# Loading and splitting the expert weights during the image attention instead of the linear attention

## The reference

```python
h = image_attention(x)                                  # 4 x 256 x 192
h = concatenate([h, txt], axis=1)                       # 4 x 384 x 192
h = h + linear_attention(layernorm(h))                  # q, k = elu(..)+1, gate, running sum of k (x) v, head norm
f = layernorm(h)
probs = softmax(f @ router_w.T); topk_probs, topk_idx = top_k(probs, 2)
outs  = einsum('tei,ehi->teh', silu(einsum('th,eih->tei', f, w1)), w2)
h = h + sum over the two chosen experts of balanced[k] * outs[topk_idx[k]]
```

## Time and profile before

| what | value |
|---|---|
| time, median of 3 runs | 404.68 us (402.76 to 408.04) |
| span of the profiled execution, first to last instruction | 391.4 us |
| median less span: what lies around it | 13.3 us |
| busy in the span: PE, DVE, ACT, POOL | 65%, 67%, 47%, 33% |
| mean granted TensorE clock | 0.711 |

### The profile page before, as it was taken

The page is one execution under the profiler, slowest core; times in us unless marked ns, Lnnn a source line. Parts: engine busy times, 40 slices in busy tenths (PEclk is TensorE's granted clock), DMA queues, the critical chain, the costliest instruction groups (busy, mean ns, idle before and its releaser), DMA issues.

```text
span 391.4 us, 7182 instructions
## 1 busy us (share of the span) xinstructions
PE 254.3 (65%) x2269; PEld 182.2 (47%) x2270; DVE 261.5 (67%) x763; ACT 184.2 (47%) x396; POOL 128.6 (33%) x133
## 2 busy tenths in 40 slices
PE   5986658776443334546656579512899999999800
PEld 3444434444343333435555457501376667667600
DVE  2115568997388898899949976597355555655566
ACT  1131325898798587657526321400255456445401
POOL 3000232554025423303300000012667876866321
PEclk9998556999555565555555555555699999999975
DMA  6000032000004512220100000000211211110046
GB/s 182 6 0 0 1 124 93 3 0 2 2 2 107 121 68 83 80 82 2 32 1 3 7 23 3 30 30 10 62 51 51 69 45 57 53 43 27 26 146 216
DMA packets 12973, 18.98 MB, mean 48 GB/s; under 512 B 3259, under 2 KB 10850, under 8 KB 12434
## 3 DMA queue, kind: packets, MB, share of 16 engines
q1 hardware_dynamic: 9922, 13.90, 11.8%
q0 software_dynamic: 3024, 4.73, 4.1%
HBM read 14.68 MB, written 5.41 MB: 51 GB/s over the span
## 4 chain that ended last, share of the span: by engine, by line
PE 43%; DVE 39%; issue 7%; ACT 6%; DMA 3%; SPq 1%; POOL 0%; DVEq 0%; POOLq 0%; ACTq 0%
DVE at_half L1434 6%; DVE atm L1397 5%; PE bank L891 4%; PE bank L880 3%; PE bank L904 2%; PE bank L906 2%; PE bank L905 2%; PE bank L741 2%; PE bank L876 2%; PE bank L578 2%; PE bank L879 2%; PE bank L878 2%; PE bank L877 2%; DVE v L1320 2%; PE bank L546 2%
## 5 line engine op out<-in xcount | busy, mean ns | idle before, releaser
L480 POOL TENSOR_TENSOR wx<-early,wx 128x1536 f16<-128x1536 f32 (+2 forms) x8 | 28.7, 3584 | 62.6 <-ACT wx L1075 62.6
L1116 ACT ACTIVATE qk<-bank 128x512 f32<-128x512 f32 x31 | 18.5, 597 | 65.1 <-PE bank L880 65.1
L487 POOL DMA_INDIRECT qk<-x_rows,tok_row x32 | 38.6, 1206 | 24.1 <-DVE tok_row L1550 12.8
L741 PE MATMUL bank<-vg,at_half 128*128 128x17 f16 x432 | 13.5, 176 | 40.8 <-DVE at_half L1434 40.8
L492 POOL DMA_INDIRECT y_rows<-qk,dst_row x31 | 31.4, 1013 | 21.7 <-DVE qk L1589 14.9
L1583 DVE COPY qk<-bank 128x512 f16<-128x512 f16 x31 | 13.2, 425 | 33.2 <-PE bank L891 33.2
L741 PEld LDWEIGHTS bank<-vg,at_half 128*128 128x128 f16 x432 | 12.5, 104 | 42.4 <-DVE at_half L1434 27.7
L904 PE MATMUL bank<-wx,qk 128*128 x124 | 30.5, 246 | 0.7 <-DVE qk L1583 0.5
L906 PE MATMUL bank<-wx,qk 128*128 x124 | 30.5, 246 | 0.0
L905 PE MATMUL bank<-wx,qk 128*128 x124 | 30.5, 246 | 0.0
L1056 ACT ACTIVATE at_half<-atm 128x384 f16<-128x384 f32 x48 | 22.5, 518 | 12.9 <-DVE atm L1397 12.9
(11 more groups left out here) (297 smaller groups left out, 737.0 us busy)
## 6 DMA issues: line engine op xcount, KB each, us to landing
early<-in_w SPq DMA_DIRECT2D x4, 768.0 KB, 4.2
early<-in_w1a SPq DMA_DIRECT2D x2, 1024.0 KB, 6.0
early<-in_w1b SPq DMA_DIRECT2D x4, 512.0 KB, 6.3
x_rows<-xr SPq DMA_DIRECT2D x12, 96.0 KB, 1.7
v<-y_rows SPq DMA_DIRECT2D x4, 288.0 KB, 5.0
qk<-y_rows SPq DMA_DIRECT2D x4, 288.0 KB, 5.3
out<-h SPq DMA_DIRECT2D x4, 288.0 KB, 2.9
at_half<-in_wq SPq DMA_DIRECT2D x1, 704.0 KB
```

Of the source, the lines that this page charges most:

```text
L480: pool.tensor_tensor(low, w, high, ALU.subtract).then_inc(s_w_low, 1)
L487: pool.indirect_dma_start(xg[:, i % 4, :], None, x2_dram, bass.IndirectOffsetOnAxis(ap=tok_row[:, i:i + 1], axis=0), bounds_check=NTOK - 1 ...
L741: mm = pe.matmul(bank[6][:, hh * VE:(hh + 1) * VE], at_half[:, a_, i, g, :], vg[:, t * H + hh, v, :], start=(c == 0 and hh == 0 and a_ == ...
```

## The change

Four stages take the place of two, and none of them lies in `early`: they are the places of `v32` (the values), `vg` (their halves), and the last two pieces of 2048 words of `qk` (queries and keys). All of these are written only in the projections. So the loads need to wait for nothing: SP issues the first four jobs directly behind the setup loads, the others when the job of four before is subtracted, and only then places the bias rows. ACT rounds each job in the image attention in one pass (scale and cast together). POOL now scales in place and then subtracts, for the jobs 0 to 3 ahead of the qkv low halves, for 4 to 6 ahead of `x_low(0)`, and for 7 between `x_low(1)` and `x_low(2)`. The subtraction of the jobs 2 and 3 covers 128 partitions as the others do. New waits: ACT waits for six subtractions before the projections, and for eight before tile 6 of them; DVE for six before it sets the ones and zeros of `vg`, which move from the start to tile 2; ACT for all key halves before the linear attention.

```diff
+NB = 4
+FREE_V = 6
+FREE_QK = 8
...
+        stage = (v32[:].rearrange("p t e -> p (t e)"), vg_words[:],
+                 late[:, T * H * SLOT - 2 * STG:T * H * SLOT - STG], late[:, T * H * SLOT - STG:T * H * SLOT])
...
-            sp.wait_ge(s_himg_mm, B)
             for n, (kind, e0) in enumerate(jobs):
-                if n >= 2:
-                    sp.wait_ge(s_w_low, n - 1)
+                if n >= NB:
+                    sp.wait_ge(s_w_low, n - NB + 1)
...
+            def expert_weights(n):
+
+                w, high, low = staged(n)
+                pool.wait_ge(s_w_high, n + 1)
+                link(pool.tensor_scalar(w, w, WS, None, ALU.mult))
+                pool.tensor_tensor(low, w, high, ALU.subtract).then_inc(s_w_low, 1)
+
+            for n in range(4):
+                expert_weights(n)
             pool.wait_ge(s_wqhigh_ready, 2)
...
+            for n in range(4, 7):
+                expert_weights(n)
...
             x_low(0)
             x_low(1)
+            expert_weights(7)
...
-            for n in range(len(jobs)):
-                w, high, low = staged(n, parts[jobs[n][0]][1])
-                pool.wait_ge(s_w_high, n + 1)
-                pool.tensor_tensor(low, w, high, ALU.subtract).then_inc(s_w_low, 1)
...
+            def expert_weights(n):
+
+                w, high, _low = staged(n)
+                act.wait_ge(s_w_loaded[n % NB], 16 * loads[n])
+                act.activation(high, w, ACT.Copy, scale=WS).then_inc(s_w_high, 1)
+
             softmax(0)
             softmax(1)
+            expert_weights(0)
+            expert_weights(1)
             for b in range(B):
                 himg(b)
                 if b + 2 < B:
                     softmax(b + 2)
+                if b == 0:
+                    expert_weights(2)
...
+                expert_weights(b + 3)
...
+            expert_weights(7)
+            act.wait_ge(s_w_low, FREE_V)
             for t in range(T + 2):
                 if t < T:
+                    if t == (T * H * SLOT - 2 * STG) // (H * SLOT):
+                        act.wait_ge(s_w_low, FREE_QK)
...
-                    act.activation(w, w, ACT.Copy, scale=WS).then_inc(s_w_scaled, 1)
...
-                    act.wait_ge(s_w_scaled, t + 1)
-                    act.activation(high, w, ACT.Copy).then_inc(s_w_high, 1)
...
+                if t == 2:
+                    dve.wait_ge(s_w_low, FREE_V)
+                    link(dve.memset(vg[:, :, 0, DH:VE], 1.0))
+                    link(dve.memset(vg[:, :, 1, DH:VE], 0.0))
```

More of the change, by code:

```diff
@@ L119, in build @@
         xp1 = qkT[:].rearrange("p a n -> p (a n)")[0:NP1, 0:B * NI]
-        early = sb("early", [P, 2 * STG])
-        stage = early[:].rearrange("p (b n) -> p b n", b=2)
+        early = sb("early", [P, 4 * IT * NI + B * IT * D])
         atm = sb("atm", [P, HG, G, P])
@@ L163, in build @@
         v32 = sb("v32", [P, T * H, DH])
-        vg = sb("vg", [P, T * H, 2, VE], F16)
+        vg_words = sb("vg", [P, T * H * VE])
+        vg = vg_words[:].bitcast(F16).rearrange("p (t v e) -> p t v e", v=2, e=VE)
         state = sb("state", [P, G * HG * VE])
@@ L304, in build @@
         s_x2_stored = [sem(f"x2_stored{i}") for i in range(2)]
-        s_w_loaded = [sem(f"w_loaded{i}") for i in range(2)]
-        s_w_scaled = sem("w_scaled")
+        s_w_loaded = [sem(f"w_loaded{i}") for i in range(NB)]
         s_w_high = sem("w_high")
@@ L353, in build @@
         jobs = [(k, e0) for k in parts for e0 in range(0, E, STG // parts[k][0])]
-        loads = [sum(2 if k == "w1b" else 1 for k, _ in jobs[n % 2:n + 1:2]) for n in range(len(jobs))]
+        loads = [sum(2 if k == "w1b" else 1 for k, _ in jobs[n % NB:n + 1:NB]) for n in range(len(jobs))]
+        assert len(jobs) == FREE_QK and all(n % NB > 1 for n in range(FREE_V, FREE_QK))
         def staged(n, rows=P):
@@ L360, in staged @@
             ne = STG // width
-            return (stage[0:rows, n % 2, 0:ne * width].rearrange("p (e c) -> p e c", c=width),
+            return (stage[n % NB][0:rows, 0:ne * width].rearrange("p (e c) -> p e c", c=width),
                     by_expert[0:rows, e0:e0 + ne, high:high + width], by_expert[0:rows, e0:e0 + ne, low:low + width])
@@ L404, in _ @@
                     for r in range(2):
-                        sp.dma_start(stage[r * 64:(r + 1) * 64, n % 2, 0:cols], w).then_inc(s_w_loaded[n % 2], 16)
+                        sp.dma_start(stage[n % NB][r * 64:(r + 1) * 64, 0:cols], w).then_inc(s_w_loaded[n % NB], 16)
                 else:
-                    sp.dma_start(stage[:, n % 2, 0:cols], w).then_inc(s_w_loaded[n % 2], 16)
+                    sp.dma_start(stage[n % NB][:, 0:cols], w).then_inc(s_w_loaded[n % NB], 16)
+            sp.wait_ge(s_wqhigh_ready, 2)
+            sp.wait_ge(s_biaslow_ready, 1)
+            for v in range(2):
+                sp.dma_start(w_half[D - P + v:D - P + v + 1, 1, 1, 0:3 * D], bias_half[:, v, :]).then_inc(s_bias_placed, 16)
             for t in range(T):
@@ L1048, in _ @@
             heads_t(1)
+            act.wait_ge(s_klow_ready, T)
             for t in range(T + 1):
@@ L1062, in _ @@
                     heads_t(t + 1)
-                if t < len(jobs):
-                    w, high, _low = staged(t)
-                    act.wait_ge(s_w_loaded[t % 2], 16 * loads[t])
-                    act.activation(w, w, ACT.Copy, scale=WS).then_inc(s_w_scaled, 1)
                 if 0 <= t - 4 < PT:
@@ L1181, in _ @@
             dve.memset(oT[DC:DC + 1, :, :, :], 1.0).then_inc(s_ones_ready, 1)
-            link(dve.memset(vg[:, :, 0, DH:VE], 1.0))
-            link(dve.memset(vg[:, :, 1, DH:VE], 0.0))
             dve.wait_ge(s_axt_mm, 1)
```

1 line of the change is left out of this document (removed).

## The result

| | before | after |
|---|---|---|
| time, median of 4 runs each, taken together | 404.66 us (402.76 to 408.04) | 435.79 us (435.22 to 437.54) |
| ratio, 95% interval | | 1.0758 (1.0687 to 1.0828) |
| span of the profiled execution | 391.4 us | 434.0 us |

The change makes the kernel 31.1 us slower. The forecast, 419 (404 to 431), has the sign and not the size.

What follows compares the result with a forecast made beforehand. VectorE (DVE) was taken to bound the linear attention, a chain of turns the image attention. Queue 14.2 + waits 13 + memsets 0.4 - linear attention 12.9 = +14.7 us, giving 419 us; 8 of 10 within 404 to 431.

Steps and rivals of the forecast that it cites:

- Part 1: Linear attention: eight subtractions leave GpSimd and VectorE's waits on them go, a gain of 12.9 us.
- Part 2: GpSimd's queue before the projections: scales of 2.0 and 1.55 us plus subtractions start `x_low(0)` at 70.7, 14.2 us later.
- Part 3: Image attention and norm chains: VectorE and GpSimd hold each other up in four places, 13 us together (0 to 17).
- job 7: Beside the second norm chain: its scale and subtraction stop the chain for most of 1.55 + 3.10, 2.5 us.
- The 3.5 us of the norm chain: First norm chain: its 17 instructions move one per GpSimd instruction; some fourteen left when GpSimd ends, some 3.5 us.
- The rest: Loads, ScalarE's first passes and its new waits cost nothing; VectorE's two memsets moved into the projections cost 0.4 us.
- The place of `x_low(0)` before: End of the image attention: GpSimd's first `x_low` read at 56.55 us, the start the delay was counted from.
- The 13.3 us between median and span: Whole kernel: time taken to lie around the 391.4 us span, added to the predicted span of 406.1 to give 419.4.
- Rival B: GpSimd's queue: the scale is as slow as the subtraction, 12.9 us more, 432 us; chance 0.13.
- A: Image attention: VectorE's waits cost nothing extra, GpSimd's queue alone decides, 406.4 us, no change; chance 0.22.
- C: Linear attention: a faster TensorE there; chance 0.10, a third of it together with A.
- D: Start of kernel: early loads come late, sharing rings with the setup; 4 us late gives 423 us; chance 0.05.

Runs made afterwards that it cites:

- e12: Kernel after, with GpSimd's scale replaced by a copy of the weights onto themselves: 406.52 us, ratio 1.0291 to the kernel before.
- e3: Kernel after without GpSimd's scale and subtractions, low halves set to zero in the setup: 392.25 us, ratio 0.9643 to the kernel before.
- e4: Kernel before without its eight subtractions, low halves set to zero in the setup: 393.26 us, ratio 0.967.
- e5: Kernel before, with each GpSimd subtraction cut in four instructions: 404.33 us, ratio 0.9943.
- e6: Also called the probe: kernel before plus seven GpSimd instructions on scratch, from 4.6 to 33.8 us; one run, 406.32 us, span 404.3.
- e10: Kernel before plus five unused subtractions on GpSimd from 27 us on; one run, 404.44 us against 396.42.
- e11: Kernel before plus four unused scales on GpSimd from 27 us on; one run, 407.79 us against 396.42.
- e13: Kernel after with the scale on GpSimd left out, so GpSimd only subtracts: 395.96 us, ratio 1.0015 to the kernel before.
- e9: Kernel before, with jobs 0 to 5 loaded early, cast by ScalarE in one pass, low halves made by VectorE while waiting for TensorE: 385.82 us, ratio 0.9738.
- e8: Kernel after, with GpSimd's scales and subtractions replaced by zero fills of about the same length: 422.51 us, ratio 1.0673 to the kernel before.
- e7: Kernel after, with each GpSimd scale and subtraction cut in four: 438.31 us, ratio 1.0861 to the kernel before.

## Why the prediction was wrong in size

By its own steps, each against the stages above:

- **Part 1, what goes from the linear attention: right.** Predicted -12.9, measured -13.0. L1320, L1325, L1361 and L1358 of the earlier trace rows are at 0.75 and 0.17 us. All of it was on the chain.
- **Part 2, GpSimd's queue in front of `x_low(0)`: the step that failed.** Its words: "From above, it should not be longer than the subtraction with two inputs, 4.07. I take 2.0 and 1.55". The scale took 5.37 and 4.08. That is 4 x 3.37 + 3 x 2.53 = 21.1 us more, and with 0.08 between each scale and its subtraction, seven times, 21.6: the queue's work ends at 92.4 without its pauses, not at 70.7. The bound was argued from the number of inputs. The only rows of GpSimd with one stream were fills, and the copy is indeed near them. An arithmetic operation with one input was not in the rows, and "from above" should have stayed open. The prediction had named this as a sign of being wrong: "if the scale takes under 1.5 or over 3 us".
- **Part 3, the waits in the image attention: right for the kernel that it thought of, hidden in the one that came.** It had 4 + 3 + 3.5 = 10.5 us of pauses in GpSimd's queue, and 2.5 for job 7. e12, where the second operation costs what was assumed, has 2.94 + 2.96 + 2.85 = 8.8, and 2.9 in the second norm chain, so each of the four was near by itself and not only their sum. The kernel after has 3.7, since the longer queue covers them. Job 7 beside the second norm chain was given 2.5 us and took 5.5: a scale and a subtraction of 7.25 us instead of 4.65, and the two stalls of 2.95 in L1242 and L1178. The 3.5 us of the norm chain rest on all 17 of its instructions waiting; that was an assumption, and no row of before shows it for a small one with two inputs. The pause there was 2.85 us in e12. In the kernel after L1188 at 84.42 and L1191 at 91.63 have two inputs and took 2.95 and 2.97 us, each until a subtraction ended.
- **The rest.** The two fills on VectorE were 0.4 and are within the +0.9 of their stage. Loads, ScalarE's passes and SP's waits cost nothing, as e3 shows (`x_low(0)` at 59.67, e4 59.66).
- **The place of `x_low(0)` before.** It was read as 56.55, which is right for that one execution. The four kernels with no weight work of GpSimd there (e3, e4, e5, e6) have it at 59.7 to 60.8. Against the probe's 60.41 the queue displaced 3.9 us less than was counted. Most of it is TensorE's: L593, L596 and the first L578 take 3.36 + 0.74 + 1.50 = 5.6 us on the chain of before, the same matmuls in e4 4.18 + 1.37 + 2.83 = 8.4, at a granted clock that both profiles give as 1.00 from 24 to 35 us. What made the difference stays open.

The sum again, from 14.7: scale +21.6, pauses 3.7 - 10.5 = -6.8, job 7 +3.0, place of `x_low(0)` -3.9, and the three stages behind +0.5 - 0.1 + 0.6. That is 29.6 us. The stages against the probe give 29.7, the times 31.1. And e12 puts the sum with the price that it assumed to the test: 10.6 us slower, a ratio of 1.0291 (to 1.0344), where the forecast was 14.7 and 419.4 / 404.7 = 1.036. Of the 4.1 between, 3.1 are the place of `x_low(0)` before (56.55 against 59.67). The 13.3 us between median and span stood on both sides of the forecast and cancel in it.

Rival B had this mechanism, a scale as slow as the subtraction, at 432, and was given 0.13. That it comes so near is partly luck: the scale was slower than B has it (5.4 against 4.07), and B kept all 13 us of part 3, of which 3.7 + 5.5 came. A, waits that cost nothing, is refuted by e12 (8.8 us of pauses, ratio 1.0291) and by e10 and e11: waits do come through where the queue leaves room. In the kernel that came the queue was so full that A is nearer there than the forecast, 3.7 us against 10.5. C, which had 0.10, was a faster TensorE in the linear attention; the granted clock there stays at 0.53, against 0.52. D is refuted by e3, which has the early loads and loses nothing (ratio 0.9643, e4 0.967).

## What to carry to other kernels

Work moved into the idle time of an in-order engine must be summed with a measured price for every kind of operation. If the trace has no row for one, put it alone into a probe, or keep the bound from above open and give that side its chance. Idle time of GpSimd is not free for VectorE: in e10 and e11 idle work there, over before anything was due, made the kernel 8.0 and 11.4 us slower. In front of a chain of small VectorE instructions the same subtractions cost as much as they did where they came from (e13, ratio 1.0015). What helped (e9) was to give the work to VectorE itself, in gaps where it waited for TensorE. When queue and waits overlap, test them apart: idle work shows the waits, and a row of three prices shows how much of each is hidden.

## What the runs showed of the hardware

- GpSimd's tensor_scalar with a constant, 128x2048 f32: 5.36 to 5.38 us, 2.6 ns a column, in place or not, f32 or f16 out. A multiplication of two f32 tensors: 4.50. The subtraction with one f16 input: 4.07. A copy: 1.89. A fill: 3.50 for 4096 columns.
- GpSimd's subtraction held VectorE's small tensor_scalars (after, L1178 at 102.19: 2.96 us, 0.17 in the probe) and its small instructions with two inputs (after, L1191 at 91.63: 2.97 us, else 0.19). Fills held the tensor_scalars as well, up to 1.94 us where five fills took 9.67 (e8, L1238), and none of the small ones with two inputs (0.18 us).
- GpSimd's work took longer in pieces: four scales of 512 columns 5.87 us, one of 2048 5.38; four subtractions 4.50, one 4.05 (e7, after).
- The maximum over `bank`, which VectorE reads from PSUM, went on beside GpSimd's work: it took 0.68 us under a running scale (e11, at 43.62), and 0.69 with GpSimd idle (56.71).
- The same low half took VectorE 2.29 us (e9, with the scale in the same instruction) and GpSimd 5.38 + 4.05 (after).
